# Swin block on one Trainium2 core: second MLP layer as three half-precision products, input load moved to GpSimd's queue, a copy moved to ScalarE

## Chip, cores and metric

The kernel runs on one core of a Trainium2 chip. The metric is the device time of one launch in microseconds (us); the median of several runs is compared. The profiler names the engines PE (TensorE), ACT (ScalarE), DVE (VectorE), POOL (GpSimd) and SP (SyncE, which here only issues DMAs).

## What is computed

A shifted-window attention block (Swin) on x of 32 x 56 x 56 x 128 in float32, with windows of 7 x 7 tokens, shift 3, 16 heads of 8, and an MLP of width 512:

```
y = roll(layernorm(x, g1, b1), (-3, -3))             # then cut into 32*64 windows of 49 tokens
q, k, v = split(yw @ qkv_w.T + qkv_b)                # 16 heads of 8
attn = softmax(q*scale @ k.T + bias[rel] + mask)
o = (attn @ v) @ proj_w.T + proj_b                   # windows put back, rolled by (3, 3)
x = x + o
h = gelu(layernorm(x, g2, b2) @ fc1_w.T + fc1_b)
out = x + h @ fc2_w.T + fc2_b
```

## The kernel before

The work is cut into 128 bands: a band n is one row of 8 windows in each of two images (784 tokens, 7 x 112). The program is a software pipeline over steps t: in step t the engines work on band t+2 (load and first layernorm), t+1 (projections, row maxima of the logits), t (attention), t-1 (output projection, second layernorm) and t-2 (MLP). The order on every engine is written out by hand in a function `body` per engine; engines wait for one another by semaphores alone, so an instruction that waits holds everything behind it on its engine. All DMAs of the loop are issued by SP, in one queue, also in written order. A DMA signal counts only when the data have landed.

TensorE, in one step: the last `pv` of band t-1; transposes of z2 and z1 (L838, L846); a small transpose of the maxima; three token rows of the second MLP layer `fc2` of the band before (L821, FC2_PARTS[0]); `fc1` halves around the q and k projections (L805, L867); the spreading of the softmax denominators (L881); the v projection (L895); the output projection (L904); and then a loop over the 8 windows w: `logits` (L771, L776), in even w from 2 on `pv` (L791), in odd w one token row of `fc2`, and `max_logits` of the next band (L741). `max_logits` of window 0 waits until VectorE has written x1 (L681), because both use the same PSUM banks.

VectorE, in one step: low halves of h, y; reciprocals; the last rows of the output (`finish`, L581); statistics of the loaded x (L521, L527), which wait for the DMA of x; the low halves of k and q (L641), which the v projection on TensorE waits for (both in the same PSUM bank); oT (L657), which the output projection waits for; a copy of values (`v_own`, L672); x1; the fourth copy of values (L687); then eight row maxima (L589) with the statistics of x1 between them.

GpSimd, in one step: splitting of the reciprocals (L372 to L378), two additions of biases over 896 columns (L384 for x_res, L391 for x1_b), and two layernorms (`norm`).

ScalarE copies and casts out of PSUM, and computes gelu (L438) and the exponentials (L421); gelu writes `hid`, a tile of its own in float32, 128 x 784 for each of 4 chunks. `fc2` multiplies `hid` by `w_2` in float32; the compiler makes two matmul instructions of each float32 one. The other MLP layer already works on halves: a float32 operand a is kept as a_hi + a_lo, both float16, and a product is a_hi b_hi + a_lo b_hi + a_hi b_lo.

```
def finish(n, p, edge):        # VectorE: adds ps and x1_b, waits for fc2 of this part
def exp_pair(n, w):            # ScalarE: exponentials of window w into probs[.., w % 4, ..]
```

Of the kernel before, what the change touches and what calls it, by code (L numbers as in the profile page):

```python
# [29 lines left out]
F16 = mybir.dt.float16  # L30
# [41 lines left out]
def swin_block_kernel(nc, x, wqT, wkT, wvT, wvpT, wpT, w1T, w2T, cols, rows, table_k, table_q, ident, eye,  # L72
# [11 lines left out]
    with ctx:  # L84
# [5 lines left out]
        w_2 = sb("w_2", [C, CH, C])  # L90
# [45 lines left out]
        hid = sb("hid", [C, CH, WS * TP])  # L136
# [4 lines left out]
        w_1, bv_wide = hid[:, 3, 0:HID], hid[:, 3, HID:HID + TP]  # L141
        w_q, w_k, w_v, w_vp = (oT_raw[:, k // 3, (k % 3) * C:(k % 3 + 1) * C] for k in range(4))
# [5 lines left out]
        def tokens_of(bank):  # L148
# [9 lines left out]
         s_h_lo, s_fc1, s_gelu, s_fc2, s_fin, s_stored, s_bd1, s_bd2, s_zero, s_init, s_initp, s_inita, s_bt,  # L158
# [11 lines left out]
                "h_high_ready", "h_low_ready", "fc1_done", "gelu_done", "fc2_done", "y_ready", "y_stored",  # L170
# [46 lines left out]
        def _(sp):  # L217
            band_dmas(sp, xr, x_in, 0, False, False, s_x)
# [30 lines left out]
            def body(t, edge, odd):  # L249
# [8 lines left out]
                n = t + 2  # L258
                if exists(n) and n != 0:

                    sp.wait_ge(s_t1, n)
                    band_dmas(sp, xr, x_in, n, edge(n), False, s_x)
# [70 lines left out]
        def _(pool):  # L333
            for dst, src in ((idn, ident), (own, own_rows), (is_part, parts), (sel, spread)):
                pool.dma_start(dst[:, :], src).then_inc(s_const, 16)
# [29 lines left out]
            def body(t, edge, odd):  # L365
                n = t - 1
                if exists(n):

                    pool.wait_ge(s_rsum, n + 1)
# [10 lines left out]
                    if n == 0:  # L380
                        pool.wait_ge(s_w, 16 * N_W)
                        pool.wait_ge(s_init, 2)
                    pool.wait_ge(s_xres_dma, loads(n, edge(n)))
                    nc.gpsimd.tensor_tensor(x_res[:, :, :], x_res[:, :, :],  # L384
                                            proj_b[:, :].unsqueeze(1).to_broadcast([TP, WS, C]),
                                            ALU.add).then_inc(s_xres, 1)
                n = t - 2
                if exists(n):
                    if past(n, 0):
# [3 lines left out]
                                            ALU.add).then_inc(s_x1b, 1)  # L393
                n = t + 2
# [10 lines left out]
        def _(act):  # L405
# [27 lines left out]
            def gelu(n, c):  # L433
                if c == 0 and past(n, 0):
                    act.wait_ge(s_fc2, 2 * n)
# [5 lines left out]
            def body(t, edge, odd):  # L441
# [537 lines left out]
```

## Time and profile before

| | before |
|---|---|
| median of 3 runs | 4084.6 us (4084.42 to 4090.56) |
| the profiled execution, its time | 4095.41 us |
| its span, first to last instruction | 4093.6 us |
| granted TensorE clock, mean | 0.995 |
| busy: PE, DVE, ACT, POOL | 96%, 70%, 65%, 49% |

A busy share says how long an engine had something in work, as a mean over stages; who sets the pace is read from who waits for whom, and where in a step.

### The profile page before, as it was taken

To read this page: it belongs to the slowest core of one execution; us is meant where nothing else is said; L and a number is where in the kernel's file an instruction comes from. 1 tells how busy PE (TensorE), PEld (TensorE's weight loads), DVE (VectorE), ACT (ScalarE), POOL (GpSimd) and SP (SyncE) were. 2 spreads that over 40 slices of the span, in tenths; PEclk is the share of its full clock that TensorE was granted. 3 is DMA by queue.
4 is the path that set the end of the run, shared out by engine and by line. 5 is a ranking of instruction groups with operands and counts; after the bars stand their busy time and mean duration, and the time that the engine had idled before them with its cause. 6 is when DMAs were issued, how large, how long until landed. Compare 5 with 4: busy or idle time off the path is not lost. (4 is left out here: it accounts for less than half of the span.)

```text
span 4093.6 us, 168809 instructions
## 1 busy us (share of the span) xinstructions
PE 3947.3 (96%) x72080; PEld 3111.1 (76%) x72080; DVE 2855.1 (70%) x7453; ACT 2674.9 (65%) x3712; POOL 2002.3 (49%) x3476
## 2 busy tenths in 40 slices
PE   3899999999999999999999999999999999999998
PEld 2677777777777777777777777777777777777776
DVE  6677677677767777776776776777777667677764
ACT  1666666666666666666766666666666666666664
POOL 4454545445455454544544544454454445445453
PEclk8999999999999999999999999999999999999999
DMA  2333333333333333333333333333333333333332
GB/s 77 100 108 115 109 109 112 110 105 112 114 106 110 113 111 110 111 113 105 112 114 105 110 114 110 109 111 108 108 109 117 106 109 112 112 105 109 112 109 60
DMA packets 609568, 441.49 MB, mean 108 GB/s; under 512 B 142083, under 2 KB 608371, under 8 KB 608819
## 3 DMA queue, kind: packets, MB, share of 16 engines
q1 hardware_dynamic: 608355, 428.88, 35.6%
q8 instruction: 569, 9.32, 1.0%
q0 software_dynamic: 464, 1.81, 0.2%
q14 instruction: 180, 1.47, 0.1%
HBM read 106.14 MB, written 51.46 MB: 38 GB/s over the span
## 5 line engine op out<-in xcount | busy, mean ns | idle before, releaser
L589 DVE TENSOR_REDUCE neg_max<-ps 113x16 f32<-113x784 f32 x1024 | 995.9, 973 | 760.7 <-PE ps L741 760.5
L421 ACT ACTIVATE probs<-ps 113x784 f32<-113x784 f32 x1024 | 844.6, 825 | 858.4 <-PE ps L776 855.7
L821 PE MATMUL ps<-w,hid 128*112 128x128 f32 x7168 | 933.5, 279 | 1.9 <-ACT hid L438 1.0
L821 PEld LDWEIGHTS ps<-w,hid 128*112 128x112 f32 x7168 | 818.4, 177 | 81.9 <-issue 79.4
L776 PE MATMUL ps<-st_q,st_k 128*49 128x196 f16 x8192 | 696.2, 249 | 0.0
L771 PE MATMUL ps<-bias,eye_k 106*64 106x392 f16 x4096 | 686.5, 331 | 0.0
L438 ACT ACTIVATE hid<-ps,col 128x784 f32<-128x784 f32 x512 | 468.1, 915 | 165.4 <-PE ps L805 144.2
L741 PE MATMUL ps<-mx_k,mx_q 128*49 128x196 f16 x8192 | 544.2, 253 | 31.7 <-DMA mx_q<-q_hi 20.0
L350 POOL TENSOR_SCALAR ve<-mv 112x7 f32<-112x7 f32 x256 | 54.4, 212 | 1048.4 <-DVE mv L527 903.1
L776 PEld LDWEIGHTS ps<-st_q,st_k 128*49 128x49 f16 x8192 | 446.9, 105 | 122.0 <-issue 0.5
L372 POOL TENSOR_SCALAR r_hi<-sums 128x98 f16<-128x98 f32 x128 | 36.5, 285 | 897.9 <-DVE sums L630 897.9
L791 PE MATMUL ps<-probs,v_own 113*32 113x49 f32 x32768 | 464.4, 209 | 1.8 <-issue 1.5
L791 PEld LDWEIGHTS ps<-probs,v_own 113*32 113x32 f32 x32768 | 393.2, 110 | 83.6 <-issue 82.8
L741 PEld LDWEIGHTS ps<-mx_k,mx_q 128*49 128x49 f16 x8192 | 313.1, 103 | 152.1 <-DMA mx_q<-q_hi 33.1
L361 POOL TENSOR_SCALAR x_in<-x_in,rs,nm 112x128 f32<-112x128 f32 x896 | 389.5, 451 | 13.5 <-POOL nm L356 0.4
L361 POOL TENSOR_SCALAR z<-x,rs,nm 112x128 f32<-112x128 f32 x896 | 388.5, 449 | 13.4 <-POOL nm L356 0.3
L352 POOL TENSOR_TENSOR rs<-ve,half 112x7 f32<-112x7 f32 x256 | 380.4, 1486 | 21.3
L429 ACT ACTIVATE pv_sb<-ps 128x392 f32<-128x392 f32 x512 | 255.6, 499 | 203.9 <-PE ps L791 192.4
L414 ACT ACT_TABLE_LOAD x253 | 324.6, 1283 | 4.5
L521 DVE BATCH_NORM_STATS2 st<-x_in 112x6 f32<-112x128 f32 x896 | 185.9, 279 | 201.8 <-DMA x_in<-in_x 201.8
L384 POOL TENSOR_TENSOR x_res<-x_res,proj_b 112x896 f32<-112x896 f32 x128 | 267.2, 2088 | 10.3
L391 POOL TENSOR_TENSOR x_b<-x,fc_b 112x896 f32<-112x896 f32 x128 | 267.1, 2087 | 5.6 <-DVE y_out L581 5.6
(109 smaller groups left out, 6502.4 us busy)
## 6 DMA issues: line engine op xcount, KB each, us to landing
st_k<-k_hi SPq DMA_DIRECT2D x256, 196.0 KB
st_q<-q_hi SPq DMA_DIRECT2D x1024, 49.0 KB
oT_raw<-pv_sb SPq DMA_DIRECT2D x256, 196.0 KB, 3.6
x_in<-in_x SPq DMA_DIRECT2D x224, 196.0 KB
x_res<-in_x SPq DMA_DIRECT2D x224, 196.0 KB
out_y<-y_out SPq DMA_DIRECT2D x224, 196.0 KB
mx_k<-k_hi SPq DMA_DIRECT2D x512, 49.0 KB
mx_q<-q_hi SPq DMA_DIRECT2D x128, 196.0 KB
```

The source lines that it names most:

```text
L352: nc.gpsimd.tensor_tensor(rs[:, :], ve[:, :], half[:, :], ALU.pow).then_inc(s_rs, 1)
L361: last = nc.gpsimd.tensor_scalar(z[:, i, :], src[:, i, :], rs[:, i:i + 1], nm[:, i:i + 1], ALU.mult, ALU.add)
L384: nc.gpsimd.tensor_tensor(x_res[:, :, :], x_res[:, :, :], proj_b[:, :].unsqueeze(1).to_broadcast([TP, WS, C]), ALU.add).then_inc(s_xres, 1)
L414: nc.scalar.activation(scrap[:, :], col[0:1, 0:1], function)
L421: nc.scalar.activation(probs[0:KP, w % 4, :].rearrange("p (b c) -> p b c", b=2), ps[0:KP, b:b + 2, 0:HB * WT], ACT.Exp).then_inc(s_exp, 1)
L438: nc.scalar.activation(hid[:, c, :].rearrange("p (b q) -> p b q", b=2), ps[:, bank:bank + 2, 0:HT], ACT.Gelu, bias=col[:, BF + c:BF + c + ...
L589: nc.vector.tensor_reduce(neg_max[0:KP, :, :, w].rearrange("p e g -> p g e"), ps[0:KP, 0:2, :].rearrange("p b (g c) -> p (b g) c", g=2)[:, ...
L741: last = mm(group(im, 0, g, 256), mx_q[edge(n)][:, g, span], mx_k[:, g, :, span], start=True, stop=True)
L771: mm(ps[HP * im:HP * (im + 1), bank + b, 0:HB * WT], eye_k[0:BIAS_ROWS, kind, im, :], bias[0:BIAS_ROWS, b, :], start=True, stop=False)
L776: last = mm(group(im, bank, g, EQ * WT), st_k[par][:, g, span], st_q[par][:, :, g, span], start=False, stop=(g % 2 == 1))
L791: last = mm(ps[32 * r:32 * r + VC, 6, first:first + WT], v_own[0:KP, w, h, :], probs[0:KP, w % 4, h * WT:(h + 1) * WT], start=True, stop=True)
L821: last = mm(ps[0:TP, 7, (i - first) * C:(i - first + 1) * C], hid[:, c, i * TP:(i + 1) * TP], w_2[:, c, :], start=(c == 0), stop=(c == CH ...
```

## The change

Three things are changed.

1. `fc2` works on halves. The weights are scaled by 64 and split once at the start (`w2_hi`, `w2_lo`). VectorE casts each chunk of the gelu's output to float16 (`hid_high`, four casts of 128 x 784), GpSimd subtracts the cast from it (`hid_lo`, four subtractions of 128 x 784), and TensorE does three float16 products where one float32 product stood (two of its instructions). The gelu's float32 output no longer has a tile of its own but lies in `probs`, so the first four exponentials of a step wait for GpSimd's four subtractions, and `fc2`'s first row in a step waits for the casts and the subtractions. `finish` scales by 1/64 in the same instruction.
2. The load of x is issued by GpSimd instead of SP, after x_res's bias addition, which moves up to the start of GpSimd's step. It waits as before for the transposes of the z1 whose tile it overwrites.
3. The fourth copy of values moves from VectorE, after x1, to ScalarE, between the exponentials of windows 0 and 1.

```diff
-        w_2 = sb("w_2", [C, CH, C])
+        w2_hi, w2_lo = (sb(n, [C, CH, C], F16) for n in ("w2_hi", "w2_lo"))
-        hid = sb("hid", [C, CH, WS * TP])
+        hid_hi, hid_lo = (sb(n, [C, CH, WS * TP], F16) for n in ("hid_hi", "hid_lo"))
+        hid = probs
 @block.sync
-                    sp.wait_ge(s_t1, n)
-                    band_dmas(sp, xr, x_in, n, edge(n), False, s_x)
 @block.gpsimd
+                    pool.wait_ge(s_xres_dma, loads(n, edge(n)))
+                    nc.gpsimd.tensor_tensor(x_res[:, :, :], x_res[:, :, :],
+                                            proj_b[:, :].unsqueeze(1).to_broadcast([TP, WS, C]),
+                                            ALU.add).then_inc(s_xres, 1)
+                n = t + 2
+                if exists(n) and n != 0:
+                    pool.wait_ge(s_t1, n)
+                    band_dmas(pool, xr, x_in, n, edge(n), False, s_x)
...
+                    for c in range(CH):
+                        pool.wait_ge(s_hid_hi, CH * n + c + 1)
+                        nc.gpsimd.tensor_tensor(hid_lo[:, c, :], hid[:, c, :], hid_hi[:, c, :],
+                                                ALU.subtract).then_inc(s_hid_lo, 1)
 @block.scalar, exp_pair
+                if w < CH and exists(n - 2):
+                    act.wait_ge(s_hid_lo, CH * (n - 2) + w + 1)
 @block.scalar, body
                         exp_pair(t, w)
+                        if w == 0:
+                            nc.scalar.activation(v_place(0, 1), v_made(0, 1), ACT.Copy).then_inc(s_vown_b, 1)
 @block.vector
+            def hid_high(n, c):
+                dve.wait_ge(s_gelu, CH * n + c + 1)
+                if c == 0 and past(n, 0):
+                    dve.wait_ge(s_fc2, 2 * n)
+                nc.vector.tensor_copy(hid_hi[:, c, :], hid[:, c, :]).then_inc(s_hid_hi, 1)
...
-                    dve.wait_ge(s_v, 2 * n + 2)
-                    nc.vector.tensor_copy(v_place(0, 1), v_made(0, 1)).then_inc(s_vown, 1)
 @block.tensor, fc2
-                    last = mm(ps[0:TP, 7, (i - first) * C:(i - first + 1) * C], hid[:, c, i * TP:(i + 1) * TP], w_2[:, c, :],
-                              start=(c == 0), stop=(c == CH - 1))
+                    for w_part in (w2_hi, w2_lo):
+                        mm(row, hid_hi[:, c, i * TP:(i + 1) * TP], w_part[:, c, :],
+                           start=(c == 0 and w_part is w2_hi), stop=False)
+                for c in range(CH):
+                    if i == first and p == 1:
+                        pe.wait_ge(s_hid_lo, CH * n + c + 1)
+                    last = mm(row, hid_lo[:, c, i * TP:(i + 1) * TP], w2_hi[:, c, :], start=False, stop=(c == CH - 1))
```

On VectorE, before, from the statistics of the loaded x to the first row maximum of a step:

```order
L521 BN_STATS st<-x_in 112x6 x7
L527 BN_AGGR mv<-st 112x2 x7
L641 SCALAR_TENSOR_TENSOR k_lo<-ps,col,k_hi 128x8x49 x2
L641 SCALAR_TENSOR_TENSOR q_lo<-ps,col,q_hi 128x8x49 x2
L657 TENSOR_TENSOR oT<-oT_raw,ps 128x7x49 x2
L657 TENSOR_TENSOR oT<-oT_raw,ps 128x14x4
L657 TENSOR_TENSOR oT<-oT_raw,ps 128x14x3
L672 COPY v_own<-ps 49x512
L681 TENSOR_TENSOR x<-ps,x_res 112x512
L681 TENSOR_TENSOR x<-ps,x_res 112x384
L687 COPY v_own<-ps 49x512
```

The same place on VectorE in the changed kernel (`hid` is called `probs` there):

```order
L534 BN_STATS st<-x_in 112x6 x7
L540 BN_AGGR mv<-st 112x2 x7
L605 CAST hid_hi<-probs 128x784 x2
L666 SCALAR_TENSOR_TENSOR k_lo<-ps,col,k_hi 128x8x49 x2
L666 SCALAR_TENSOR_TENSOR q_lo<-ps,col,q_hi 128x8x49 x2
L682 TENSOR_TENSOR oT<-oT_raw,ps 128x7x49 x2
L682 TENSOR_TENSOR oT<-oT_raw,ps 128x14x4
L682 TENSOR_TENSOR oT<-oT_raw,ps 128x14x3
L605 CAST hid_hi<-probs 128x784 x2
L700 COPY v_own<-ps 49x512
L709 TENSOR_TENSOR x<-ps,x_res 112x512
L709 TENSOR_TENSOR x<-ps,x_res 112x384
```

Two casts now stand ahead of k_lo and two between oT and the first value copy; the copy behind x1 is gone.

On GpSimd, before, one whole step from the splitting of the reciprocals:

```order
L372 TENSOR_SCALAR r_hi<-sums 128x98
L375 TENSOR_TENSOR sums<-sums,r_hi 128x98
L378 TENSOR_SCALAR r_lo<-sums 128x98
L384 TENSOR_TENSOR x_res<-x_res,proj_b 112x896
L391 TENSOR_TENSOR x_b<-x,fc_b 112x896
L350 TENSOR_SCALAR ve<-mv 112x7
```

The same place on GpSimd in the changed kernel:

```order
L370 TENSOR_TENSOR x_res<-x_res,proj_b 112x896
L208 DMA x_in<-in_x 56x7x128 x2
L384 TENSOR_SCALAR r_hi<-sums 128x98
L387 TENSOR_TENSOR sums<-sums,r_hi 128x98
L390 TENSOR_SCALAR r_lo<-sums 128x98
L396 TENSOR_TENSOR x_b<-x,fc_b 112x896
L403 TENSOR_TENSOR hid_lo<-probs,hid_hi 128x784 x4
L347 TENSOR_SCALAR ve<-mv 112x7
```

The bias addition and the load stand ahead of the reciprocals, and the four subtractions ahead of the first layernorm.

## Rows read from the trace of the kernel before

**Rows 1.** The page: busy time, share of the span and instructions by engine.
```profile
PE 3947.3 (96%) x72080; PEld 3111.1 (76%) x72080; DVE 2855.1 (70%) x7453; ACT 2674.9 (65%) x3712; POOL 2002.3 (49%) x3476
```

**Rows 2.** Who waited for whom: us in total, times, longest us.
```profile
DVE st L521 <- DMA x_in<-in_x: 201.8, 128, 2.8
...
PEld ps L895 <- DVE q_lo L641: 73.4, 127, 2.7
...
PEld ps L741 <- DMA mx_q<-q_hi: 33.1, 55, 5.0
```

**Rows 3.** Line 449, which runs once a step: duration in ns, first and last start.
```profile
L449 ACT ACTIVATE h_hi<-ps x128: 824/824/825, 138.9 to 4073.2; 128x784 f16<-128x784 f32 x128
```

**Rows 4.** VectorE's timeline in one step: start, us, what, idle before it.
```profile
2006.17 0.49 DVE L581 TENSOR_TENSOR y_out<-ps,x_b 112x384 f32<-112x384 f32 x1
2008.05 1.45 DVE L521 BATCH_NORM_STATS2 st<-x_in 112x6 f32<-112x128 f32 x7 [1.39 <-DMA x_in<-in_x]
...
2010.03 1.13 DVE L641 SCALAR_TENSOR_TENSOR k_lo<-ps,col,k_hi 128x392 f16<-128x392 f32 x2
2011.08 1.15 DVE L641 SCALAR_TENSOR_TENSOR q_lo<-ps,col,q_hi 128x392 f16<-128x392 f32 x2
2012.34 1.17 DVE L657 TENSOR_TENSOR oT<-oT_raw,ps 128x343 f32<-128x343 f32 x4
2013.42 1.06 DVE L672 COPY v_own<-ps 49x512 f32<-49x512 f32 x1
2014.85 1.16 DVE L681 TENSOR_TENSOR x<-ps,x_res 112x512 f32<-112x512 f32 x2 [0.36 <-PE ps L904]
```

**Rows 5.** TensorE's timeline in the same step.
```profile
2002.24 0.83 PE L846 MATMUL ps<-idn,x_in 112*128 112x112 f32 x7
...
2016.15 0.53 PE L741 MATMUL ps<-mx_k,mx_q 128*49 128x196 f16 x8
...
2017.29 1.13 PE L821 MATMUL ps<-w,hid 128*112 128x128 f32 x8
2018.35 0.53 PE L741 MATMUL ps<-mx_k,mx_q 128*49 128x196 f16 x8
```

**Rows 6.** The chain that ended last, in order of time: start, us, what.
```profile
3994.45 2.62 PE ps L821 x24
...
4003.52 1.45 PE ps L895 x24
```

**Rows 7.** Groups by shape: count, busy us, mean ns, idle before.
```profile
L564 DVE CAST hid<-hid 128x784 f16<-128x784 f32 x1 | 0.6, 568 | 0.0
L553 DVE CAST wk_hi<-oT_raw 128x128 f16<-128x128 f32 x1 | 0.2, 227 | 0.0
L375 POOL TENSOR_TENSOR sums<-sums,r_hi 128x98 f32<-128x98 f32 x128 | 47.5, 371 | 10.7
L384 POOL TENSOR_TENSOR x_res<-x_res,proj_b 112x896 f32<-112x896 f32 x128 | 267.2, 2088 | 10.3
L500 ACT ACTIVATE v_own<-ps 49x512 f32<-49x512 f32 x256 | 263.7, 1132 | 9.2 <-PE ps L895 7.5
```

**Rows 8.** VectorE's timeline in the set-up.
```profile
21.12 14.30 DVE L546 COPY v_own<-own 113x128 f32<-113x128 f32 x2 [8.50 <-DMA fc_b<-in_rows]
```

**Rows 9.** GpSimd's timeline in the set-up.
```profile
20.17 10.58 POOL L341 MEMSET st_q<- 128x12544 f16 x1
...
32.44 2.74 POOL L344 MEMSET st_k<- 128x3136 f16 x1
```

**Rows 10.** GpSimd's timeline in the step of rows 4.
```profile
2007.53 2.09 POOL L384 TENSOR_TENSOR x_res<-x_res,proj_b 112x896 f32<-112x896 f32 x1
...
2027.11 3.04 POOL L361 TENSOR_SCALAR z<-x,rs,nm 112x128 f32<-112x128 f32 x7
```

**Rows 11.** SP's queue in the same step: start and us of the issuing instructions.
```profile
2003.51 1.06 SPq L206 DMA_DIRECT2D x_in<-in_x  x2
```

**Rows 12.** DMA issues: count, KB each, median us from issue to landing.
```profile
r_rows<-r_hi SPq DMA_DIRECT2D x128, 24.5 KB, 2.2
...
own<-in_own_rows POOLq DMA_DIRECT2D x1, 1.0 KB, 3.3
```

More of the change, by code:

```diff
@@ L333, in _ @@
         def _(pool):
+            band_dmas(pool, xr, x_in, 0, False, False, s_x)
             for dst, src in ((idn, ident), (own, own_rows), (is_part, parts), (sel, spread)):
@@ L367, in body @@
                 if exists(n):
+                    if n == 0:
+                        pool.wait_ge(s_w, 16 * N_W)
+                        pool.wait_ge(s_init, 2)
+                    pool.wait_ge(s_xres_dma, loads(n, edge(n)))
[6 more added lines that the diff above has]
+                    band_dmas(pool, xr, x_in, n, edge(n), False, s_x)
+                n = t - 1
+                if exists(n):
                     pool.wait_ge(s_rsum, n + 1)
@@ L379, in body @@
                                             ALU.mult, ALU.add).then_inc(s_r_lo, 1)
[L380 to L386, printed above, removed]
                 n = t - 2
@@ L433, in gelu @@
             def gelu(n, c):
-                if c == 0 and past(n, 0):
-                    act.wait_ge(s_fc2, 2 * n)
                 act.wait_ge(s_fc1, CH * n + c + 1)
@@ L560, in _ @@
             then(nc.vector.tensor_tensor(w1_lo[:, :], w_1, w1_hi[:, :], ALU.subtract))
+            then(nc.vector.tensor_scalar(w_2, w_2, W_SCALE, None, ALU.mult))
+            then(nc.vector.tensor_copy(w2_hi[:, :, :], w_2))
+            then(nc.vector.tensor_tensor(w2_lo[:, :, :], w_2, w2_hi[:, :, :], ALU.subtract))
             then(nc.vector.tensor_tensor(proj_b[:, :], proj_b[:, :], bp_ps, ALU.add))
@@ L580, in finish @@
                 dve.wait_ge(s_fc2, 2 * n + 2 - p)
-                nc.vector.tensor_tensor(y_out[:, i0:i1, :],
-                                        ps[0:TP, 7, 0:(i1 - i0) * C].rearrange("p (i c) -> p i c", c=C),
-                                        x1_b[:, i0:i1, :], ALU.add).then_inc(s_fin, 1)
+                nc.vector.scalar_tensor_tensor(
+                    y_out[:, i0:i1, :], ps[0:TP, 7, 0:(i1 - i0) * C].rearrange("p (i c) -> p i c", c=C),
+                    1 / W_SCALE, x1_b[:, i0:i1, :], ALU.mult, ALU.add).then_inc(s_fin, 1)
+            def hid_high(n, c):
[3 more added lines that the diff above has]
+                nc.vector.tensor_copy(hid_hi[:, c, :], hid[:, c, :]).then_inc(s_hid_hi, 1)
             def row_maxima(n, w):
@@ L635, in body @@
                     norm1(n, edge)
+                if exists(t - 2):
+                    hid_high(t - 2, 0)
+                    hid_high(t - 2, 1)
                 n = t + 1
@@ L665, in body @@
                         r[:, :, last_w, :, kept:WS].rearrange("p m i j -> p i m j")).then_inc(s_oT, 1)
+                if exists(t - 2):
+                    hid_high(t - 2, 2)
+                    hid_high(t - 2, 3)
                 n = t
@@ L782, in pv @@
                 if u == 0:
-                    pe.wait_ge(s_vown, 2 * n + 2)
-                    pe.wait_ge(s_vown_b, 2 * n + 2)
+                    pe.wait_ge(s_vown, n + 1)
+                    pe.wait_ge(s_vown_b, 3 * (n + 1))
                 else:
@@ L811, in fc2 @@
                 if i == first and p == 1:
-                    pe.wait_ge(s_gelu, CH * (n + 1))
+                    pe.wait_ge(s_hid_hi, CH * (n + 1))
                     if exists(n + 2):
-                        pe.wait_ge(s_vown, 2 * (n + 2) + 1)
-                        pe.wait_ge(s_vown_b, 2 * (n + 2) + 1)
+                        pe.wait_ge(s_vown, n + 3)
+                        pe.wait_ge(s_vown_b, 3 * (n + 2) + 1)
                     elif n > 0:
@@ L819, in fc2 @@
                     pe.wait_ge(s_fin, 2 * n + 1)
+                row = ps[0:TP, 7, (i - first) * C:(i - first + 1) * C]
                 for c in range(CH):
-                    last = mm(ps[0:TP, 7, (i - first) * C:(i - first + 1) * C], hid[:, c, i * TP:(i + 1) * TP], w_2[:, c, :],
-                              start=(c == 0), stop=(c == CH - 1))
+                    for w_part in (w2_hi, w2_lo):
[5 more added lines that the diff above has]
+                    last = mm(row, hid_lo[:, c, i * TP:(i + 1) * TP], w2_hi[:, c, :], start=False, stop=(c == CH - 1))
                 if i == end - 1:
```

12 lines of the change are left out of this document (5 added, 7 removed).

## Prediction, made before the changed kernel ran

> **What bounds the kernel now.** I read the busy shares first. TensorE is in work 96% of the span and the others 49 to 70% [rows 1], so the first guess is that the kernel is as long as TensorE's instructions, and that whatever shortens them shortens the kernel. A busy share does not say that nothing else is tight, so I read the waits next. One stands out for its count: TensorE's first weight load of the v projection waits for VectorE's q_lo in 127 of 128 steps, 73.4 us in all, 0.58 a step. And VectorE itself sits idle in 128 of 128 steps for the DMA of x, 201.8 us, 1.58 a step [rows 2]. So in the middle of each step there is a second chain, and TensorE comes to it only half a microsecond early: transposes of z1, DMA of x, statistics, k_lo, q_lo, v projection. The line that runs once a step starts at 138.9 and for the 128th time at 4073.2: 3934.3/127 = 30.98 us a step [rows 3].
>
> VectorE's timeline shows that chain. It finishes the output rows at 2006.66, idles until x lands, begins the statistics at 2008.05, k_lo at 2010.03, ends q_lo at 12.23, oT follows at 12.34, the value copy at 13.42, and x1 ends at 16.01, with only 0.36 idle in it (times from here on without the 2000) [rows 4]. TensorE's row maxima of window 0 wait for x1; they start at 16.15 [rows 5]. From 8.05 to 16.01 VectorE has 0.36 us to spare: whatever is put on VectorE there comes out at 16.15 later, nearly one to one. After 16.15 TensorE sets the pace, with VectorE idle before its row maxima.
>
> **The change, part by part.** All terms are for one step.
>
> *fc2 on TensorE.* Now a row of fc2 is 8 float32 instructions; from its start at 17.29 to the next max_logits at 18.35 it takes 1.06 [rows 5]. Three rows in one go take 2.62 for 24 [rows 6]. In the changed kernel a row is 12 float16 products of 128 columns. The nearest row is the v projection: 24 float16 products of 128 columns in 1.45 [rows 6], 0.060 each, so a row costs 0.70 to 0.73; I take 0.70. The four rows in the window loop save 4 x 0.36 = 1.44, the three ahead of fc1 save 2.62 - 36 x 0.060 = 0.46. The 0.46 falls ahead of the v projection, where TensorE waits for q_lo already: worth nothing as long as the VectorE chain is late. The 1.44 lies behind x1 and counts in full.
>
> *Two casts ahead of k_lo.* A cast of 128 x 784 from float32 to float16 took 568 ns [rows 7]. Two: **+1.14** on q_lo. Nothing hides them but VectorE's idle time ahead of x, and they stand behind that wait, not in it: the same x holds them.
>
> *Two casts between oT and the value copy.* Another 1.14, of which the 0.36 idle time before x1 takes its part: +0.78 from q_lo to x1.
>
> *The casts against GpSimd.* In the set-up VectorE starts two copies of 113 x 128 elements at 21.12 and they end only at 35.42 [rows 8], though a cast of 128 x 128 takes 0.23 [rows 7]. GpSimd's memsets began at 20.17 and the last ended at 35.18 [rows 9]. So a copy from SBUF to SBUF on VectorE stood still while GpSimd worked, through several back-to-back instructions. The Trainium skill (SBUF — State Buffer, Who interferes with whom) has the rule behind it: such copies and casts use the port pair that VectorE shares with GpSimd, it is locked for the whole instruction, and the later one blocks fully. This trace agrees, and adds that a queue of GpSimd work is not let in between. By the rule the casts may block; without it they cost their 0.57 only.
>
> What GpSimd does then: a subtraction costs between 371 ns for 98 columns and 2088 for 896 [rows 7]; along that line (2.15 ns a column) 784 columns cost 1.85. With x landing 0.4 late (below), the first two casts run 10.48 to 11.62, GpSimd subtracts two chunks from 11.65 to 15.35, and VectorE wants its third cast at 10.48 + 4.48 = 14.96: **+0.4** of blocking. The bound below is 0 (no lock); the bound above is that GpSimd slips in between the two casts of a pair, 1.85 - 0.57 = +1.3. GpSimd waits for a signal from the first cast while the second stands ready on VectorE, so I don't take that.
>
> *x loaded by GpSimd.* SP issued at 3.51 [rows 11] and x was there at 8.05 [rows 4]. GpSimd can issue once the z1 transposes end at 3.07 [rows 5], provided x_res's addition is done (2.09 us [rows 10], and x_res is loaded at the end of the step before): some 0.2 to 0.4 earlier. The only price for its queue is from the set-up: 3.3 us to landing for 1 KB against 2.2 for SP's 24.5 KB [rows 12], +1.1, beside other traffic. So x moves by -0.3 (no surplus) to +1.0 (whole surplus, more if 392 pieces per DMA take GpSimd long to describe). I take **+0.4**. The Trainium skill (DMA: Bandwidth & Descriptors, Specifications) states about 1 us to the first byte on GpSimd's path and about 0.6 on SP's. By that alone x would land about 0.1 to 0.2 late, and the sum would be some 30 us smaller.
>
> *x_res's addition* moves ahead of the reciprocals, where GpSimd idles; x1_b's addition comes 2.09 earlier and would end at 9.62 instead of 11.68 [rows 10]. Hidden. SP's queue gets 1.06 shorter [rows 11], which brings the operands of max_logits no later; with max_logits itself 2 us later, the waits for mx_q (33.1 us [rows 2]) go: **-0.2**.
>
> *The fourth value copy on ScalarE.* It costs 1.13 [rows 7] behind exponential 0. Exponential 1 waits for logits 1, which come behind max_logits of window 0; as that is held by x1 there are about 2 us of cover. If x1 were not late, exponential 1 would be about 0.8 late, and the cover behind it (fc2, maxima, logits: 0.7 + 0.36 + 0.8) still takes it. Nothing. On VectorE the copy stood behind x1, where VectorE has idle time afterwards: nothing gained.
>
> *The new waits.* The third and fourth subtraction: casts end at 16.5, subtractions at 18.35 and 20.2. fc2's first row starts near 19.95 and needs the last one 0.45 later: just met. Behind them stand GpSimd's two layernorms. z2 is ready at 30.15 now [rows 10] and would be about 2 us later, as x1 and its statistics are (less two shorter fc2 rows). It is wanted just ahead of the next z1 transposes, which stand at 2.24 [rows 5] and so at 33.2 a step later, and move by 1.08 themselves. Just met, too.
>
> **Sum.** x1 ends at 16.01 + 0.4 + 1.14 + 0.78 + 0.4 = 18.73: +2.72. Loop -1.44, mx_q -0.2. Net +1.08 a step, over 126 full steps +136 us; the three set-up instructions for w2 +2. The profiled execution took 4095.4 (span 4093.6), 10.8 above the median of the runs, so 4095.4 + 138 - 10.8 = 4222. I forecast **4220 us**, 3.3% slower, own range 4080 to 4300 (x at -0.3 and no lock: -1.1 a step, -139 us; x at +1.0: +0.6 a step, +76 us).
>
> **The rivals.**
>
> *A. The saving arrives.* If the VectorE chain had slack that I don't see, the kernel is as short as TensorE's work: 1.44 + 0.46 + 0.2 = 2.1 a step, 4084.6 - 126 x 2.1 + 2 = 3822. For it: 96% busy [rows 1]. Against: q_lo waited for in 127 of 128 steps [rows 2], and 2.28 us of casts put into that chain. Chance 0.07.
>
> *B. x lands early (faster or level).* VectorE idles 1.39 before x [rows 4]. If GpSimd's load landed that much earlier, and there were no lock, the net is 1.14 - 1.39 + 0.78 - 1.44 - 0.2 = -1.11, 140 us faster: 3947. It decides at x landing 0.28 earlier without a lock. With the lock the first cast can't start before x1_b's addition ends at 9.62, 0.46 before now, and the best is 1.14 - 0.46 + 0.78 + 0.4 - 1.44 - 0.2 = +0.22: about 4112. For it: a queue of its own, not behind SP's sums. Against: rows 12. Chance 0.17 for faster (3920 to 4075), 0.05 for level.
>
> *C. GpSimd becomes the bound.* It gets 4 x 1.85 and two DMA issues more per step. If subtractions take 2.4 instead of 1.85, or GpSimd takes the ports between paired casts (+1.3), fc2's first row waits, z2 comes late: +1.3 x 126 = 164 us more, 4385. For it: the two margins above are 0.2 and 1. Chance 0.15.
>
> *D. The forecast* has the rest, 0.56.
>
> **Numbers.** Leaving out A and a part of B below, and half of C above, the range is 3970 to 4360. What a measurement of this kernel can tell from no change is about 0.2%, 8 us. Faster: A, B and the tail of D, 0.27; same 0.05; slower 0.68.
>
> **What the profile after would show.** The cast ahead of k_lo at 0.57 each; TensorE's wait for q_lo grown from 0.58 to about 2 us a step; max_logits of window 0 waiting for x1; fc2's rows at 0.70; a step of about 32 us; TensorE's share near 88%. The x step is wrong if VectorE's wait for x is under 1.2 us a step; the lock is wrong if the third cast is never over 0.6 us. The forecast falls if VectorE's chain from q_lo to x1 takes under 4 us, or x lands a microsecond sooner.

## The result, and the profile after

| | before | after |
|---|---|---|
| median, 4 runs each | 4087.58 us | 4430.18 us (4424.05 to 4444.72) |
| ratio of the medians | | 1.0833, interval 1.0810 to 1.0856 |
| the profiled execution, its time and span | 4095.41, 4093.6 | 4444.72, 4442.8 |
| granted TensorE clock, mean | 0.995 | 0.949 |

The kernel became 343 us slower. The sign was forecast, the size was not: 4220 was said, and 4430 lies outside the range.

The page of the changed kernel, busy time by engine, and the granted clock of TensorE in 40 equal slices:

```profile
PE 3934.8 (89%) x75664; PEld 3121.4 (70%) x75664; DVE 2978.4 (67%) x7840; ACT 2785.0 (63%) x3840; POOL 3144.3 (71%) x4276
...
PEclk8999999999999999999999999999999999999998
```

TensorE was to get shorter by 1.9 us of work a step, some 240 us; its busy time fell by 12.5 [rows 1]. A matmul that runs at the lower clock is busy for longer, so a busy time that does not fall as the work does is the first sign of the clock. (Experiment 12 below issues as many instructions on TensorE, 75664, at a granted clock of 0.993, and there TensorE is busy for 3755.2 us.)

The line that runs once a step, in the changed kernel:

```profile
L460 ACT ACTIVATE h_hi<-ps x128: 823/823/823, 147.0 to 4415.0; 128x784 f16<-128x784 f32 x128
```

(4415.0 - 147.0)/127 = 33.61 us a step against 30.98 [rows 3]: **+2.63 a step, 334 us**. The first start is 8.1 us later, and from the last start to the end of the span it is 27.8 against 20.4; 334 + 8.1 + 7.4 is the 349 us between the spans.

Who waits for whom in the changed kernel (us in total, times, longest):

```profile
POOL hid_lo L403 <- DVE hid_hi L605: 392.5, 252, 3.9
DVE st L534 <- DMA x_in<-in_x: 382.7, 128, 5.6
...
PE ps L911 <- DVE k_lo L666: 341.5, 126, 5.2
...
DVE x L709 <- PE ps L934: 130.6, 130, 2.0
...
PEld ps L925 <- DVE q_lo L666: 115.2, 127, 4.2
```

VectorE's wait for x went from 1.58 to 2.99 us a step [rows 2]. TensorE now waits already for k_lo, one instruction ahead of the v projection (the spreading of the denominators, L911, is late too), 2.71 a step, and then for q_lo. And x1 (L709) waits a microsecond a step for the output projection, where it had waited less than half of that in the kernel before:

```profile
DVE x L681 <- PE ps L904: 58.6, 129, 1.8
```

So VectorE waits for TensorE behind the point where TensorE waited for VectorE.

VectorE's timeline in one step of the changed kernel (start, us, what, idle before it):

```profile
1999.97 0.50 DVE L597 SCALAR_TENSOR_TENSOR y_out<-ps,x_b 112x384 f32<-112x384 f32 x1
2003.81 0.29 DVE L534 BATCH_NORM_STATS2 st<-x_in 112x6 f32<-112x128 f32 x1 [3.35 <-DMA x_in<-in_x]
...
2005.79 1.01 DVE L605 CAST hid_hi<-probs 128x784 f16<-128x784 f32 x2
2006.72 1.15 DVE L666 SCALAR_TENSOR_TENSOR k_lo<-ps,col,k_hi 128x392 f16<-128x392 f32 x2
2007.79 1.15 DVE L666 SCALAR_TENSOR_TENSOR q_lo<-ps,col,q_hi 128x392 f16<-128x392 f32 x2
2008.86 1.15 DVE L682 TENSOR_TENSOR oT<-oT_raw,ps 128x343 f32<-128x343 f32 x4
2009.93 1.04 DVE L605 CAST hid_hi<-probs 128x784 f16<-128x784 f32 x2
2010.88 1.07 DVE L700 COPY v_own<-ps 49x512 f32<-49x512 f32 x1
2012.83 1.16 DVE L709 TENSOR_TENSOR x<-ps,x_res 112x512 f32<-112x512 f32 x2 [0.88 <-PE ps L934]
2014.76 0.98 DVE L611 TENSOR_REDUCE neg_max<-ps 113x16 f32<-113x784 f32 x1 [0.77 <-DVE x L709]
```

From the statistics to k_lo it is 2.91 us; in [rows 4] it is 1.98. From the end of q_lo (2008.94) to x1 (2012.83) there are 3.89 us, but only 3.0 of work.

TensorE's timeline in the same step. The v projection is 24 products in a row, of which the second, the third and the last stand here, and fc2's first row of the loop begins at 2015.28:

```profile
2008.02 0.58 PE L911 MATMUL ps<-r_rows,sel 32*128 32x392 f16 x2 [3.01 <-DVE k_lo L666]
...
2009.07 0.31 PE L925 MATMUL ps<-wv_hi,yT_lo 128*128 128x128 f16 x1
2009.18 0.31 PE L925 MATMUL ps<-wv_lo,yT_hi 128*128 128x128 f16 x1
...
2011.42 0.31 PE L925 MATMUL ps<-wv_lo,yT_hi 128*128 128x128 f16 x1
2011.53 1.82 PE L934 MATMUL ps<-w_p,oT 128*112 128x128 f32 x14
...
2014.13 0.53 PE L765 MATMUL ps<-mx_k,mx_q 128*49 128x196 f16 x8
...
2015.28 0.26 PE L847 MATMUL ps<-w_hi,hid_hi 128*112 128x128 f16 x1
...
2016.09 0.53 PE L765 MATMUL ps<-mx_k,mx_q 128*49 128x196 f16 x8
```

The products of the v projection start 0.107 us apart ((2011.42 - 2009.07)/22). Before, 24 took 1.45, 0.060 each [rows 6]. Busy time in stretches of this step (us; busy PE, PEld, DVE, ACT, POOL; then the granted clock, the DMAs' busy share, GB/s): TensorE's wait, the v projection, and what follows up to max_logits:

```profile
2005.00:2008.00 3.00, 0.01 (x1) 0.01 (x1) 2.97 (x14) 2.40 (x3) 1.60 (x1) 1.00 0.18 67
2008.00:2011.50 3.50, 3.08 (x26) 2.62 (x27) 3.50 (x9) 0.95 (x1) 2.89 (x3) 0.54 0.82 243
2011.50:2014.20 2.70, 2.70 (x31) 2.27 (x30) 1.60 (x3) 1.24 (x2) 2.63 (x2) 0.96 0.29 106
```

TensorE stood still for three microseconds, and in the stretch behind it the granted clock is 0.54, near the lower of its two levels (1.2 GHz of 2.4). In the kernel before, the same v projection ran at the upper one:

```profile
2012.28:2013.63 1.35, 1.35 (x24) 1.35 (x25) 1.29 (x5) 1.33 (x2) 1.27 (x2) 1.00 0.20 74
```

The Trainium skill (TensorE: Matmul & The Clock Gate, Part 1: The HAM clock gate) gives 107 ns from one 128-column product of 16-bit operands to the next at 1.2 GHz and 56 ns at 2.4. This trace agrees: 0.107 in the v projection, 0.05 to 0.06 in most of fc2.

GpSimd's timeline, the load of x and the subtractions:

```profile
1997.18 1.61 POOL L208 DMA_DIRECT2D x_in<-in_x  x2 [1.31 <-PE ps L876]
...
2006.40 3.55 POOL L403 TENSOR_TENSOR hid_lo<-probs,hid_hi 128x784 f16<-128x784 f32 x2 [2.97 <-DVE hid_hi L605]
2010.57 3.56 POOL L403 TENSOR_TENSOR hid_lo<-probs,hid_hi 128x784 f16<-128x784 f32 x2 [0.61 <-DVE hid_hi L605]
```

From issue to statistics the load takes 6.63 us, against 8.05 - 3.51 = 4.54 [rows 4, 11]. Issuing is itself part of it, 1.61 us for two DMAs against 1.06. The step shown is somewhat above the mean wait (3.35 against 2.99), that of [rows 4] somewhat below (1.39 against 1.58), so for the sum I take the means.

The casts and the subtractions as groups (count; busy us, mean ns; idle before):

```profile
L403 POOL TENSOR_TENSOR hid_lo<-probs,hid_hi 128x784 f16<-128x784 f32 x512 | 911.2, 1799 | 392.5 <-DVE hid_hi L605 392.5
L605 DVE CAST hid_hi<-probs 128x784 f16<-128x784 f32 x512 | 269.7, 569 | 3.7 <-ACT probs L449 3.6
```

A subtraction costs 1.80 (forecast: 1.85), and the casts take what a cast took in the set-up [rows 7]: they are almost never blocked.

**The step's budget.** x later: 2.99 - 1.58 = +1.41. Casts ahead of k_lo: 2.91 - 1.98 = +0.93. From the end of q_lo to max_logits of window 0: 14.13 - 8.94 = 5.19 against 16.15 - 12.23 = 3.92 [rows 4, 5], +1.27. From there to the start of the last `pv` (14.13 to 28.32, before 16.15 to 31.33), 14.19 against 15.18, -0.99. Sum +2.62, where +2.63 was measured. That it closes so well is partly luck, since x's term is a mean over all steps and the others are read from one step of each kernel. Which part of the 1.27 is the clock is a question for an experiment.

### The profile page after: what moved, and what is told of

Its sections match the earlier page's. It is cut to its first block and busy times, and to the rows that moved or that the text cites. A ratio compares the mean times of both kernels' runs of the same rounds, so it can differ in the third digit from the quotient of the medians.

```text
span 4442.8 us, 176877 instructions
## 1 busy us (share of the span) xinstructions
PE 3934.8 (89%) x75664; PEld 3121.4 (70%) x75664; DVE 2978.4 (67%) x7840; ACT 2785.0 (63%) x3840; POOL 3144.3 (71%) x4276
## 5 line engine op out<-in xcount | busy, mean ns | idle before, releaser
L403 POOL TENSOR_TENSOR hid_lo<-probs,hid_hi 128x784 f16<-128x784 f32 x512 | 911.2, 1799 | 392.5 <-DVE hid_hi L605 392.5
L847 PE MATMUL ps<-w_hi,hid_hi 128*112 128x128 f16 x3584 | 524.3, 227 | 4.3 <-DVE hid_hi L605 3.5
L449 ACT ACTIVATE probs<-ps,col 128x784 f32<-128x784 f32 x512 | 467.5, 913 | 89.2 <-PE ps L829 59.8
L847 PE MATMUL ps<-w_lo,hid_hi 128*112 128x128 f16 x3584 | 501.6, 220 | 0.0
L511 ACT ACTIVATE v_own<-ps 49x512 f32<-49x512 f32 x256 | 274.8, 1102 | 330.7 <-PE ps L925 319.6
L847 PEld LDWEIGHTS ps<-w_hi,hid_hi 128*112 128x112 f16 x3584 | 420.0, 131 | 84.4 <-issue 79.5
L847 PEld LDWEIGHTS ps<-w_lo,hid_hi 128*112 128x112 f16 x3584 | 421.7, 131 | 0.0
L208 POOL DMA_DIRECT2D x_in<-in_x x288 | 224.6, 781 | 221.6 <-PE ps L876 198.3
L911 PE MATMUL ps<-r_rows,sel 32*128 32x392 f16 x256 | 65.5, 336 | 345.3 <-DVE k_lo L666 341.5
```

What stands on the lines that cost most here:

```text
L403: nc.gpsimd.tensor_tensor(hid_lo[:, c, :], hid[:, c, :], hid_hi[:, c, :], ALU.subtract).then_inc(s_hid_lo, 1)
L449: nc.scalar.activation(hid[:, c, :].rearrange("p (b q) -> p b q", b=2), ps[:, bank:bank + 2, 0:HT], ACT.Gelu, bias=col[:, BF + c:BF + c + ...
L511: nc.scalar.activation(v_place(1, b), v_made(1, b), ACT.Copy).then_inc(s_vown_b, 1)
L847: mm(row, hid_hi[:, c, i * TP:(i + 1) * TP], w_part[:, c, :], start=(c == 0 and w_part is w2_hi), stop=False)
```

## The experiments

The theory: the excess over the forecast has two causes, x on GpSimd's queue costs 1.4 us a step instead of 0.4, and TensorE's longer wait lowers its clock just ahead of work that VectorE waits for. The rivals: the split of fc2 itself costs more (its casts, subtractions and waits), or VectorE's chain alone is longer and the clock is a mere accompaniment.

Ratios are to runs of the kernel before that were taken beside each group of experiments. Their medians are 4092 us for experiments 1 to 4, 4093 for 5 to 8, 4097 for 9 to 11 and 4095 for 12, where the result above has 4088, so a difference of a few us between groups says nothing. The edits are shown in part: semaphore counts, indices and the first load ahead of the loop, which follow from them, are left out, and so is the old place of a load that is moved.

**1. x back on SP.** The changed kernel, with the move of x's loads alone undone:

```diff
 @block.gpsimd
-                n = t + 2
-                if exists(n) and n != 0:
-                    pool.wait_ge(s_t1, n)
-                    band_dmas(pool, xr, x_in, n, edge(n), False, s_x)
 @block.sync, behind the issues of sums
+                n = t + 2
+                if exists(n) and n != 0:
+                    sp.wait_ge(s_t1, n)
+                    band_dmas(sp, xr, x_in, n, edge(n), False, s_x)
```

> The changed kernel with the load of x back on SP, in its old place behind the loads of the sums. Theory 1 (two late links in VectorE's chain, and a TensorE clock that falls in the wait they make): VectorE's wait for x goes from 2.99 us a step back to 1.58, which is 1.41 x 127 = 179 us, and TensorE's wait ahead of the v projection falls from 2.7 us to about 1.3, so that the granted clock stays up in part of the steps: 4130 to 4250 us, clock above 0.97. Rival (GpSimd's four subtractions or the casts hold the step, whoever loads x): 4350 us or more, and VectorE's idle time only moves elsewhere.

Measured: 4153.99 us (4140.37 to 4169.15), ratio to before 1.0154 (1.0123 to 1.0185), clock 0.981. This is within what was expected. VectorE's wait for x is 205.2 us in all, as before. Of 343 us, 276 hang on the queue that loads x. What is left over the kernel before, 62 us (1.5%), is what the split costs, together with the two small moves that stay in (the copy and x_res's addition).

**2. The split alone.** As experiment 1, and the fourth copy back on VectorE:

```diff
 @block.scalar, body
-                        if w == 0:
-                            nc.scalar.activation(v_place(0, 1), v_made(0, 1), ACT.Copy).then_inc(s_vown_b, 1)
 @block.vector, behind x1
+                    dve.wait_ge(s_v, 2 * n + 2)
+                    nc.vector.tensor_copy(v_place(0, 1), v_made(0, 1)).then_inc(s_vown, 1)
```

> Only the half-precision fc2: x loaded by SP, fourth copy of values on VectorE behind x1. Theory 1: as the kernel with x on SP, within 20 us, since the copy lies behind x1 where VectorE has idle time. Rival (the copy on ScalarE pays, because max_logits and the row maxima come earlier without it on VectorE): 50 us or more slower than the kernel with x on SP.

Measured: 4165.92 us (4162.11 to 4174.74), 1.0185 (1.0165 to 1.0206). Within 20 us of experiment 1, as expected. The 12 us between them can't be told from the spread of the runs (4140 to 4169 there, 4162 to 4175 here).

**3. x on GpSimd alone.** The kernel before, with the load of x and x_res's addition moved as in the change, and nothing else.

```diff
 @block.sync
-                    sp.wait_ge(s_t1, n)
-                    band_dmas(sp, xr, x_in, n, edge(n), False, s_x)
 @block.gpsimd, start of the step, behind the addition for x_res
+                    pool.wait_ge(s_t1, n)
+                    band_dmas(pool, xr, x_in, n, edge(n), False, s_x)
```

> The kernel before with only the load of x moved to GpSimd (behind x_res's addition, as in the change). Theory 1: x lands 1.4 us later, all of it on the chain, +179 us, and if the wait that it makes is long enough for the granted clock to fall, up to 120 us more: 4260 to 4390 us. Rival (the late x in the changed kernel comes from GpSimd being busy with the subtractions, not from its queue): 4080 to 4130 us.

Measured: 4299.59 us (4294.17 to 4324.38), 1.0522 (1.0481 to 1.0564). The moved load costs 207 us by itself, in the range expected. VectorE's timeline of this kernel, then two stretches as above, TensorE's wait and the projections behind it, then TensorE's output projection:

```profile
2010.77 1.45 DVE L524 BATCH_NORM_STATS2 st<-x_in 112x6 f32<-112x128 f32 x7 [3.51 <-DMA x_in<-in_x]
...
2018.70 0.69 DVE L684 TENSOR_TENSOR x<-ps,x_res 112x512 f32<-112x512 f32 x1 [1.69 <-PE ps L907]
```

```profile
2011.80:2015.00 3.20, 1.10 (x7) 0.28 (x5) 3.17 (x15) 2.97 (x4) 1.92 (x3) 1.00 0.17 63
2015.00:2018.50 3.50, 3.50 (x33) 3.50 (x34) 2.01 (x5) 2.01 (x2) 3.25 (x9) 0.66 0.82 244
```

```profile
2016.57 3.17 PE L907 MATMUL ps<-w_p,oT 128*112 128x128 f32 x14
```

The wait for x is 375.4 us in all, 174 more than [rows 2] has. The clock falls here too, in a kernel without any of the new casts, behind waits of 1.61 us for k_lo and 0.49 for q_lo. It falls later than in the change: most of the v projection still runs at the upper level, the output projection takes 3.17 us (1.73 in the kernel before), and x1 waits for it. So the fall comes with TensorE's wait, whatever made the wait.

**4. The copy on ScalarE alone**, in the kernel before.

```diff
 @block.vector, behind x1
-                    dve.wait_ge(s_v, 2 * n + 2)
-                    nc.vector.tensor_copy(v_place(0, 1), v_made(0, 1)).then_inc(s_vown, 1)
 @block.scalar, body
+                        if w == 0:
+                            nc.scalar.activation(v_place(0, 1), v_made(0, 1), ACT.Copy).then_inc(s_vown_b, 1)
```

> The kernel before with only the fourth copy of values moved to ScalarE between exponentials 0 and 1. Theory 1: x1 is not late here, so exponential 1 comes about 0.8 us late, and what follows it on TensorE (fc2, row maxima, logits) still covers that: 4075 to 4100 us. Rival (the cover is too short): up to 0.8 x 127 = 100 us slower, 4190 us.

Measured: 4087.52 us (4077.47 to 4100.77, 10 runs), 0.9987 (0.9970 to 1.0004): no difference, as expected.

**5. TensorE's wait filled.** The changed kernel, with 50 products of 112 columns, whose result nobody reads, where TensorE would wait for k_lo:

```diff
 @block.tensor, ahead of the spreading of the denominators
+                if exists(t - 2) and exists(t + 1):
+                    pe.wait_ge(s_gelu, CH * (t - 2) + 3)
+                    for _ in range(50):
+                        mm(ps[:, 2, 0:TP], wv_hi[:, :], wv_hi[:, 0:TP], start=True, stop=True)
```

> The changed kernel, with 50 float16 products of 112 columns added on TensorE in each step in the wait ahead of the spreading products (after the third gelu; their result is read by nobody). They should take about 2.4 us of a mean wait of 2.7. Theory 1 (the granted clock falls because TensorE waits, and the v and output projections then run at half speed on the way to x1): the clock stays at 0.98 or more, the v projection takes 1.4 us instead of 2.6, and the kernel loses 0.7 to 1.2 us a step: 4280 to 4350 us. Rival (the low clock falls in time that is covered by VectorE anyway, so only the casts and the late x count): 4400 to 4440 us.

Measured: 4301.20 us (4295.97 to 4308.18), 1.0504 (1.0476 to 1.0532), clock 0.989. Useless work made the kernel **129 us faster**. The wait for x is still 383.4 us. VectorE's timeline in the part that follows:

```profile
2017.13 1.14 DVE L666 SCALAR_TENSOR_TENSOR q_lo<-ps,col,q_hi 128x392 f16<-128x392 f32 x2
...
2021.39 1.14 DVE L709 TENSOR_TENSOR x<-ps,x_res 112x512 f32<-112x512 f32 x2
2023.29 0.97 DVE L611 TENSOR_REDUCE neg_max<-ps 113x16 f32<-113x784 f32 x1 [0.77 <-DVE x L709]
```

x1 waits for nothing now, and the granted clock stays at 1.00 though the DMA engines are nearly as busy as in the slow stretches above (0.76 here, 0.82 there), so it is not their traffic that brings it down:

```profile
2020.00:2023.00 3.00, 2.58 (x34) 2.13 (x34) 2.53 (x5) 1.99 (x3) 2.83 (x2) 1.00 0.76 221
```

From the end of q_lo to the first row maximum it is 5.02 us (2018.27 to 2023.29) against 5.82 in the changed kernel (2008.94 to 2014.76). So 0.80 of the 1.27 in the budget is the clock, and the other 0.47 I put down to the second pair of casts. The whole gain is 129/126 = 1.02 a step; where the other 0.2 lies I did not trace.

**6. The first two casts behind q_lo.** As experiment 1, and the first pair of casts moved:

```diff
 @block.vector, ahead of k_lo
-                if exists(t - 2):
-                    hid_high(t - 2, 0)
-                    hid_high(t - 2, 1)
 @block.vector, behind q_lo
+                if exists(t - 2):
+                    hid_high(t - 2, 0)
+                    hid_high(t - 2, 1)
```

> The changed kernel with x on SP, and the first two casts moved from ahead of k_lo to behind q_lo. Theory 1 (VectorE's chain up to x1 sets the step, so the place of a cast in it does not matter, but TensorE waits less ahead of the v projection): q_lo 0.93 earlier, x1 at the same time, clock a little higher: 4110 to 4155 us. Rival (what counts is q_lo, since the output projection and not VectorE holds x1): up to 0.93 x 127 = 118 us faster, 4040 us.

Measured: 4482.79 us (4482.60 to 4485.39), 1.0949 (1.0917 to 1.0981). A miss: a gain was expected, and it is 329 us slower than experiment 1. VectorE's timeline, and then GpSimd's:

```profile
2029.57 1.03 DVE L605 CAST hid_hi<-probs 128x784 f16<-128x784 f32 x2
2030.52 1.15 DVE L682 TENSOR_TENSOR oT<-oT_raw,ps 128x343 f32<-128x343 f32 x4
2031.59 2.92 DVE L605 CAST hid_hi<-probs 128x784 f16<-128x784 f32 x2
```

```profile
2030.20 7.48 POOL L403 TENSOR_TENSOR hid_lo<-probs,hid_hi 128x784 f16<-128x784 f32 x4 [3.84 <-DVE hid_hi L605]
```

The third cast comes while GpSimd subtracts, and the pair takes 2.92 instead of 1.04. This is the lock of the forecast: oT, the only work between the pairs now, is too short to keep them apart, while in the change k_lo and q_lo stand between as well. The fourth cast alone takes 2.04, begun at 2032.48 while the second subtraction ran from 2032.09 to 2034.09. TensorE now waits for x1 at the first max_logits; the same row in experiment 1 stands second:

```profile
PE ps L765 <- DVE x L709: 289.3, 125, 2.3
```

```profile
PE ps L765 <- DVE x L709: 16.7, 84, 0.3
```

That is 2.1 us a step of the 2.6 by which the step is longer than in experiment 1 ((4454.8 - 140.5)/127 against (4126.6 - 141.7)/127). From max_logits of window 0 to the start of the last `pv` nothing is lost (14.18 against 14.19). The rest I did not trace. The Trainium skill (SBUF — State Buffer, Who interferes with whom) says that such a cast and a GpSimd instruction shut each other out, and that the order of issue decides who is blocked. The trace agrees: the casts issued behind a subtraction wait, 1.9 us for the pair.

**7 and 8. Two tiles of x.** With a second `x_in`, the load of a band no longer waits for the transposes of the z1 that it would overwrite, and SP issues it at the start of its step: experiment 7 on top of experiment 1, experiment 8 on top of the kernel before.

```diff
-        x_in = sb("x_in", [TP, WS, C])
+        x_in = [sb(f"x_in{e}", [TP, WS, C]) for e in range(2)]
 @block.sync, start of the step
+                n = t + 2
+                if exists(n) and n != 0:
+                    sp.wait_ge(s_st1, n)
+                    if past(n, 1):
+                        sp.wait_ge(s_t1, n - 1)
+                    band_dmas(sp, xr, x_in[odd(2)], n, edge(n), False, s_x)
```

> The changed kernel with x on SP and with two tiles for x in turn, so that its load no longer waits for the transposes of this step and stands at the start of SP's step. VectorE's wait for x (1.6 us a step) should be gone. Theory 1: q_lo 1.4 us earlier, TensorE waits little, clock 0.99, and the saving of fc2 shows: the step is about 31.5 - 1.4 us long, 3960 to 4040 us, faster than before. Rival (GpSimd, with four subtractions in its step, now holds z1 or z2): 4100 us or more, with TensorE waiting for GpSimd's layernorms.

> The kernel before with two tiles for x in turn and the early load, nothing else. Theory 1 (TensorE comes to the v projection only half a microsecond ahead of q_lo): those 0.58 us a step go, and no more, since TensorE is then full: 4010 to 4040 us. Rival (the wait is only an artefact and is made up for elsewhere): 4080 to 4095 us.

Measured: 4062.87 us (4058.34 to 4073.28), 0.9925 (0.9897 to 0.9953), and 4065.76 us (4059.07 to 4073.52), 0.9929 (0.9901 to 0.9957). The wait for x is gone from both (at most 2.4 us in all), yet both gained less than expected, and each lies between its two expectations. In the second, VectorE now waits for ScalarE's k_hi instead, 153.5 us. In the first, the lock takes part of it. Its casts as a group:

```profile
L606 DVE CAST hid_hi<-probs 128x784 f16<-128x784 f32 x512 | 388.6, 797 | 3.6 <-ACT probs L450 3.6
```

797 ns instead of 569: the earlier casts fall on x1_b's addition on GpSimd (in one step it runs from 2024.27 to 2026.36, and the pair of casts that starts at 2025.27 takes 1.99 us). With x there in time, the kernel with the split and the one without it are level: what the split saves and what its casts cost balance.

**9. The statistics of x out of the chain.** Experiment 1 with two tiles of x and of its moments: x of band t+3 is loaded a step earlier, and its statistics stand between the row maxima of windows 4 to 6, where VectorE waits for TensorE anyway.

```diff
-                n = t + 2
-                if exists(n) and n != 0:
-                    norm1(n, edge)
 @block.vector, behind the row maximum of window w
+                    if exists(t + 3) and w in (4, 5, 6):
+                        norm1(t + 3, edge, odd(3), w - 4)
```

> From the changed kernel with x on SP: two tiles for x and two for its moments, x of band t+3 loaded where band t+2 was, and its statistics (2.0 us on VectorE) taken between the row maxima of windows 4 to 6, where VectorE idles. The two casts ahead of k_lo can then start as soon as the gelu has written. Theory 1: q_lo about 0.5 us earlier than with two tiles alone, x1 too, 3950 to 4010 us, if GpSimd does not block the casts. Rival (the ports): the second cast now meets x1_b's addition or the first subtraction on GpSimd and waits for it, over 1 us; then 4060 us or more, and casts of 2 us in the trace.

Measured: 4035.44 us (4032.22 to 4037.27), 0.9839 (0.9816 to 0.9863), between the two expectations. VectorE's timeline, and GpSimd's:

```profile
2014.24 2.31 DVE L610 CAST hid_hi<-probs 128x784 f16<-128x784 f32 x1 [0.43 <-ACT probs L450]
```

```profile
2014.04 2.09 POOL L397 TENSOR_TENSOR x_b<-x,fc_b 112x896 f32<-112x896 f32 x1
```

The mechanism of the rival is there, though the time is 25 us under the rival's: one cast in the step takes 2.31 us because GpSimd's addition began 0.2 earlier, and ends 0.4 behind it.

**10. GpSimd's load, but early.** The changed kernel with two tiles of x, which GpSimd loads at the start of its step.

```diff
 @block.gpsimd, start of the step
+                n = t + 2
+                if exists(n) and n != 0:
+                    pool.wait_ge(s_st1, n)
+                    if past(n, 1):
+                        pool.wait_ge(s_t1, n - 1)
+                    band_dmas(pool, xr, x_in[odd(2)], n, edge(n), False, s_x)
```

> The changed kernel, x still loaded by GpSimd, but with two tiles for x and the load at the start of GpSimd's step, so that its longer way no longer counts. Theory 1 (the queue costs only because the load was late): as the same kernel with the load on SP, 4063 us within 30. Rival (issuing on GpSimd costs its own 1.6 us a step on a full engine or disturbs VectorE): 4120 us or more.

Measured: 4099.99 us (4092.05 to 4106.88, 10 runs), 1.0005 (0.9991 to 1.0020): 330 us faster than the change, and level with before. VectorE hardly waits for x (10.2 us in all). Against experiment 7, which differs in the queue, 37 us remain (33 by the ratios). VectorE's wait for the DMA of the denominators, which SP issues, grew from 6.7 to 35.3 us; whether that is what the kernel lost, and why that DMA comes later, was not tested. The time lies between the two expectations: the start in time is worth most of the 276 us, the queue itself the rest.

**11. x1_b's addition behind the subtractions.** Experiment 9, and GpSimd's addition for x1_b moved behind the four subtractions, and each pair of casts waits for both of its chunks of gelu.

```diff
 @block.vector, hid_high
-                dve.wait_ge(s_gelu, CH * n + c + 1)
+                dve.wait_ge(s_gelu, CH * n + c // 2 * 2 + 2)
 @block.gpsimd, behind the four subtractions instead of ahead of them
                     nc.gpsimd.tensor_tensor(x1_b[:, :, :], x1[:, :, :],
```

> The same, and besides x1_b's addition on GpSimd moved behind the subtractions, and the casts made in pairs (the first of a pair waits for both gelus), so that no GpSimd instruction runs when a cast is due, except the second subtraction against the third cast. Theory 1 with the port lock: casts of 0.5 us, q_lo level with TensorE, x1 about 0.5 late, step about 29.5 to 30.5 us: 3850 to 3980 us, the fastest. Rival (GpSimd is full with 2.1 us more ahead of the layernorms, and z2 comes late): 4050 us or more, with TensorE waiting for z2 or z1.

Measured: 4717.20 us (4710.65 to 4722.19), 1.1504 (1.1478 to 1.1529). A miss. The casts take 568 ns, as hoped, but one of the waits of this kernel reads:

```profile
DVE x L711 <- POOL x_b L403: 546.6, 127, 5.3
```

The addition reads the old x1, and VectorE must not write the new one before it is done. I had moved it behind the place at which its input is written anew.

**12. Two tiles of x1.** Experiment 11 with the cause of that wait removed: x1 has two tiles, and the bias of fc2 is added in place.

```diff
-        x1 = sb("x1", [TP, WS, C])
-        x1_b = sb("x1_b", [TP, WS, C])
+        x1 = [sb(f"x1_{e}", [TP, WS, C]) for e in range(2)]
-                    if past(n, 0):
-                        pool.wait_ge(s_fin, 2 * n)
-                    nc.gpsimd.tensor_tensor(x1_b[:, :, :], x1[:, :, :],
+                    nc.gpsimd.tensor_tensor(x1[odd(0)][:, :, :], x1[odd(0)][:, :, :],
```

> The kernel with the statistics ahead and the casts in pairs, and besides two tiles for x1, to which fc2's bias is added in place (the tile x1_b goes), so that x1 of the next band no longer waits for that addition behind the subtractions. In the kernel without the second tile VectorE waited 546.6 us for it. Theory 1 with the port lock: no cast over 0.6 us in the median, x1 early, TensorE waits for nothing long: 3880 to 3990 us, faster than every kernel so far. Rival (GpSimd's row of subtractions, bias and two layernorms, about 20 us behind the first cast, now ends after z2 is wanted): 4035 us or more, with TensorE waiting for z.

Measured over 5 runs: **3951.66 us** (3945.42 to 3960.37), 0.9650 (0.9627 to 0.9673), clock 0.993. It is the fastest kernel of this study, 3.5% ahead of before. TensorE is busy 95% of the span. Its line once a step, and VectorE's casts in it:

```profile
L458 ACT ACTIVATE h_hi<-ps x128: 824/825/826, 139.0 to 3921.7; 128x784 f16<-128x784 f32 x128
```

```profile
L607 DVE CAST hid_hi<-probs 128x784 f16<-128x784 f32 x512 | 268.6, 567 | 187.9 <-ACT probs L447 187.9
```

(3921.7 - 139.0)/127 = 29.79 a step, 1.19 less than before, with the casts at their full speed. The time is within what was expected. The statistics ahead of time were not tried in the kernel before, so how much of the 3.5% belongs to the split stays open.

## Why the prediction was wrong in size

*The bound.* Right, as far as the change goes. VectorE's chain from x to x1 sets the middle of the step, and what is put there comes out behind it: the delays of the change were passed on whole. The reverse does not hold. To take x's 1.58 us of wait away is worth 0.2 us a step (experiment 8), since k_hi is next.

*x on GpSimd, "I take +0.4".* This step failed. It measured +1.41 in the change and (375.4 - 201.8)/128 = +1.36 in experiment 3, beyond even the bound of +1.0 that I gave. I had priced the landing by a load of 1 KB [rows 12], and had set off the 0.3 us that GpSimd could start earlier. In the step shown it starts 0.14 earlier behind the last `pv` (1994.49 to 1997.18, before 2000.68 to 2003.51), and issuing alone takes 0.55 longer. The half sentence in brackets, that 392 pieces per DMA may take GpSimd long to describe, left the bound open upwards, and the sum and the range did without it. Whether it is the number of pieces that makes the load late, no run tests. By the Trainium skill's first-byte times (DMA: Bandwidth & Descriptors, Specifications) GpSimd's path would be 0.4 slower. For this load that is far too little: the wait for x grew by more than three times as much.

*The clock.* This step was missing. The forecast itself said that TensorE's wait would grow from 0.58 to about 2 us, and then costed what follows by rows at the upper level. It costs 0.80 between q_lo and the row maxima, 1.02 a step in all (experiment 5). In the terms of the budget, x's other 1.01 and the clock's 0.80 a step lie over the forecast; the terms below give back 0.92 in casts and lock, the loop costs 0.45, and 0.2 was set down for mx_q that the budget does not show. That is 1.54 a step over 126 steps, 194 us, and with 13 for set-up and end 207 of the 210 us. With the 1.02 for the clock it would be 28 us more, so single terms are good to about 0.2 a step.

*Casts ahead of k_lo, +1.14:* measured +0.93, since a pair takes 1.01 and k_lo overlaps its end. *Casts behind oT, +0.78:* +0.47, which is what experiment 5 leaves of the 1.27.

*The lock, +0.4:* nothing in the change. The mechanism is real (experiments 6, 7 and 9 show casts of up to 2.3 us), but it had no occasion: x came so late that the casts stood clear of GpSimd's additions, and the second pair started at 2009.93, as the subtractions ended (2009.95). My sum had GpSimd start behind the second cast, 1.17 after the pair's start; it starts on the signal of the first, at 2006.40, 0.61 after it.

*fc2's row, 0.70:* 0.81 (2015.28 to 2016.09), 0.25 saved and not 0.36, so the loop gave -0.99 and not -1.44. The twelve products start 0.055 apart; the first is followed by a gap of 0.10, and the last four and what comes behind them take the rest. A mean over 24 products in a row hides what a short group pays at its edges.

*mx_q, -0.2:* the wait went, from 33.1 to 5.2 us. In the step that I compared there was none before either, so the budget does not show it, and no run tells whether the time fell with it. *The fourth copy:* nothing, right (experiments 2 and 4). *Set-up, +2:* 8.1. With the load of x alone moved, the first start is 5.5 later, so most of it is GpSimd's queue again; the end of the span, +7.4, I had not looked at.

*The rivals.* A and B did not come. C did not either: GpSimd waits for the casts (392.5 us), not the reverse. The forecast without its x term was 4170, and the kernel without it is 4154 (experiment 1); there the smaller errors cancel.

## What to carry to other kernels

Price a DMA on another queue by a load of the same shape, in the same number of pieces, and give it a head start before you judge the queue: with one tile more GpSimd's queue cost 37 us over SP's instead of 276. When a forecast makes TensorE's wait longer, cost what follows at both clock levels; if the waiting engine next waits for TensorE, the loss is on the path. And an instruction that is cheap in itself may cost four times as much where it meets GpSimd, so look at what else runs at the place to which you move it.

## What was not expected of the hardware

- A wait of about 3 us in each step of 33.6 brought the clock down for the stretch behind it (0.54), and 50 useless products in the wait brought 129 us back.
- GpSimd took 0.78 us to issue each DMA of 56 x 7 rows of x (1.61 for two, SP 1.06), and from issue to use it was 6.63 us against 4.54 in the steps shown.
- A cast of 0.57 us took 2.31 behind a GpSimd addition that had begun 0.2 us earlier, and waited it out whole.
